# Expert layer's tokens without their bias, which is added where fetched rows are turned; one list product on ScalarE; the second tile's rows turned inside the first tile's first layer

## What is computed

```
h = x @ W_in + b_in                              # 2048 tokens, 256 -> 256
t = h.reshape(B * S, -1)
logits = t @ W_gate + b_gate                     # 8 experts
probs = jax.nn.softmax(logits, axis=-1)
topv, topi = jax.lax.top_k(probs, TOP_K)         # TOP_K = 2
topv = topv / jnp.sum(topv, axis=-1, keepdims=True)
route = jnp.zeros_like(probs).at[arange[:, None], topi].set(topv)
mid = jax.nn.relu(jnp.einsum('nd,edh->neh', t, W1) + b1)   # 256 -> 1024
eout = jnp.einsum('neh,ehd->ned', mid, W2) + b2            # 1024 -> 256
out = jnp.einsum('ne,ned->nd', route, eout) @ W_out + b_out
```

## Time and profile before

| | us |
|---|---|
| median of 3 timed runs | 1483.45 (1481.06 to 1484.49) |
| profiled execution, its own time | 1474.6 |
| its span in the trace | 1472.8 |
| cross-attention block, from first to last transpose back | 964.5 to 1104.3 |
| token projection and lists on PE | 1120.8 to 1146.4 |
| first transposes of fetched rows to end of first(0) | 1156.7 to 1168.0 |
| expert tiles from first(1) to the last product | 1171.2 to 1437.9 |

### The profile page before, as it was taken

The page is one execution under the profiler, slowest core; times in us unless marked ns, Lnnn a source line. Parts: engine busy times, 40 slices in busy tenths (PEclk is TensorE's granted clock), DMA queues, the critical chain, the costliest instruction groups (busy, mean ns, idle before and its releaser), DMA issues. The chain is left out here.

```text
span 1472.8 us, 27606 instructions
## 1 busy us (share of the span) xinstructions
PE 1311.2 (89%) x9707; PEld 1036.3 (70%) x9707; DVE 1016.0 (69%) x1992; ACT 877.4 (60%) x2193; POOL 465.7 (32%) x636
## 2 busy tenths in 40 slices
PE   5989999988699999968999766689989699999997
PEld 3534444435699999856888644478877599999995
DVE  5688787816456665555777896678875588888773
ACT  4436676674466666544121466477872588888873
POOL 5312221238233333432000356422110234444320
PEclk9999999999999999988999887599998799999998
DMA  4745224000000000021000300021202567777855
GB/s 88 225 77 155 45 53 76 6 5 1 30 2 1 2 2 1 2 93 29 1 1 1 81 16 1 22 56 42 50 16 76 176 215 230 236 233 231 232 161 184
DMA packets 97922, 116.16 MB, mean 79 GB/s; under 512 B 23552, under 2 KB 83193, under 8 KB 97785
## 3 DMA queue, kind: packets, MB, share of 16 engines
q1 hardware_dynamic: 88329, 99.84, 25.1%
q0 software_dynamic: 4416, 12.06, 2.7%
q10 hardware_dynamic: 5040, 2.49, 0.7%
HBM read 88.48 MB, written 16.55 MB: 71 GB/s over the span
## 5 line engine op out<-in xcount | busy, mean ns | idle before, releaser
L827 ACT ACTIVATE sa_probs<-ps 128x512 f32<-128x512 f32 (+1 forms) x304 | 154.3, 578 | 84.3 <-PE ps L780 83.2
L851 DVE TENSOR_REDUCE sa_top<-ps 128x2 f32<-128x1024 f32 (+3 forms) x160 | 171.4, 1115 | 37.7 <-PE ps L756 24.2
L3150 ACT ACTIVATE room<-ps,cx_top 128x154 f32<-128x154 f32 x256 | 97.2, 389 | 89.8 <-DVE cx_top L3214 89.8
L2688 PE MATMUL ps<-me_h,me_w_parts 128*128 128x256 f32 x1104 | 141.4, 289 | 4.2 <-DVE me_h L2774 4.2
L2688 PEld LDWEIGHTS ps<-me_h,me_w_parts 128*128 128x128 f32 x1104 | 138.0, 194 | 5.9 <-DVE me_h L2774 4.8
L2702 PE MATMUL ps<-me_w_parts,me_mid 128*128 128x256 f32 x1104 | 136.3, 283 | 0.0
L2702 PEld LDWEIGHTS ps<-me_w_parts,me_mid 128*128 128x128 f32 x1104 | 132.5, 188 | 0.0
L3012 POOL TENSOR_TENSOR room<-room 128x512 f32<-128x512 f32 x64 | 66.7, 1043 | 169.9 <-DVE room L3222 169.8
L2769 DVE TENSOR_TENSOR me_w_parts<-me_chunk,me_w_parts 128x1024 fp32r<-128x1024 f32 x92 | 110.4, 1222 | 13.2 <-ACT me_w_parts L2730 13.2
L2753 ACT ACTIVATE me_full<-ps,me_b 128x256 f32<-128x256 f32 x184 | 95.2, 517 | 40.5 <-PE ps L2688 40.5
L2798 DVE TENSOR_TENSOR me_mid<-me_full,me_mid 128x256 fp32r<-128x256 f32 x184 | 90.1, 507 | 41.3 <-ACT me_mid L2755 39.2
(11 more groups left out here) (472 smaller groups left out, 3437.0 us busy)
## 6 DMA issues: line engine op xcount, KB each, us to landing
me_chunk<-in_L_ffn_W_dram SPq DMA_DIRECT2D x92, 512.0 KB, 4.0
sa_k<-scr_k SPq DMA_DIRECT2D x48, 128.0 KB, 4.2
sa_q<-scr_q SPq DMA_DIRECT2D x96, 64.0 KB, 4.0
cn_qd<-cn_qh SPq DMA_DIRECT2D x60, 64.0 KB, 2.1
scr_q<-room SPq DMA_DIRECT2D x6, 512.0 KB, 4.3
scr_k<-room SPq DMA_DIRECT2D x6, 512.0 KB, 4.7
me_b<-in_L_ffn_b_dram SPq DMA_DIRECT2D x23, 128.0 KB, 4.3
x<-in_x_dram SPq DMA_DIRECT2D x4, 512.0 KB, 6.3
```

Source lines behind the costliest of these rows:

```text
L827: act.activation(probs[:, step % self.PROBS, h0:h0 + many, 0:w], src[:, :, 0:w], ACT.Exp, scale=DH ** -0.5).then_inc(exped.sem, 1)
L851: dve.tensor_reduce(top2[:, k % 2, k0 // 512, h0:h0 + many, sb % HBLK], src[:, :, 0:w], AX.X, ALU.max).then_inc(freed.sem, 1)
L2688: last = pe.matmul(ps[:, MID + n % 4, 0:RT], w[:, u % 2, 0, i, DM * k + P * b:DM * k + P * b + P], h[:, u % 2, j, k, :], start=(m == 0), s ...
L3150: last = act.activation(p[:, h + i, :], ps[:, S_BANK + n % SR, M * i:M * i + M], ACT.Exp, bias=top[:, t % 2, h + i:h + i + 1], accum_out=d ...
```

## The change

Four things are done.

- **b_in leaves the projection.** The load L2080, the tiles it needs, `bias_parts` on POOL and the sixteen products L2309 go. The tokens in `moe_tokens` are without b_in.
- **b_in is added in `take`.** ACT's one copy of 128x512 becomes two of 128x256 with a bias column per half k (`ACT.Identity` with `in_bias`), DVE's one subtraction becomes two `scalar_tensor_tensor` (turned row plus bias, minus high part). The semaphores count KD = 2 per tile.
- **The list product moves.** `mp_named` half 0 is made by ACT behind the copy of tile 13 (`t == NT - 3`) and no longer by DVE. The two small products on `mp_count` stand behind tile 3, not tile 4.
- **The second tile's rows are turned earlier.** turn(1) stands ahead of block 4 of first(0) on PE, and take(1) behind block 4 of tile 0 on ACT and DVE. All later tiles keep their places.

```
-    def bias_parts(self, pool):
...
-        then(pool.tensor_copy(self.ones_r[:, :], self.ones[0:3, :]))
...
-        then(pool.tensor_tensor(self.b_parts[:, :], self.b_in[:, :], self.term[:, :], ALU.add))
...
@@ Prepare.tensor
             for k in range(KD):
-                pe.matmul(bank, front.xt[:, k, P * t:P * t + P], front.w[:, k, 0:D], start=(k == 0), stop=False)
-            pe.matmul(bank, front.ones_r[:, :], front.b_parts[:, :], start=False, stop=True).then_inc(self.s["hidden"].sem, 1)
-            if t == 4:
+                last = pe.matmul(bank, front.xt[:, k, P * t:P * t + P], front.w[:, k, 0:D], start=(k == 0),
+                                 stop=(k == KD - 1))
+            last.then_inc(self.s["hidden"].sem, 1)
+            if t == 3:
@@ Prepare.scalar
+            if t == NT - 3:
+                act.wait_ge(self.s["hot_a"].sem, self.s["hot_a"].at(1))
+                act.activation(self.named[:, :, 0, :], self.one_a[:, :, :], ACT.Copy, scale=self.front.col[:, :]
+                               ).then_inc(self.s["scaled"].sem, 1)
@@ Prepare.vector
-        dve.wait_ge(self.s["hot_a"].sem, self.s["hot_a"].at(1))
-        dve.tensor_scalar(self.named[:, :, 0, :], self.one_a[:, :, :], self.front.col[:, :], None, ALU.mult
-                          ).then_inc(self.s["scaled"].sem, 1)
@@ moe_experts, tensor
                     for b in range(HB):
                         n = HB * u + b
+                        if n == HB // 2:
+                            turn(1)
...
                 first(0)
-                turn(1)
@@ moe_experts, scalar
-                    act.activation(h[:, u % 2, 0, :, :].rearrange("p k r -> p (k r)"), ps[:, TURN[u % 2], :],
-                                   ACT.Copy).then_inc(h_high.sem, 1)
+                    for k in range(KD):
+                        act.activation(h[:, u % 2, 0, k, :], ps[:, TURN[u % 2], RT * k:RT * k + RT], ACT.Identity,
+                                       bias=in_bias[:, k:k + 1]).then_inc(h_high.sem, 1)
...
-                        if b == HB - 1 and u + 1 < TILES:
+                        if b == (HB - 1 if u else HB // 2) and u + 1 < TILES:
                             take(u + 1)
@@ moe_experts, vector
-                    dve.tensor_tensor(h[:, u % 2, 1, :, :].rearrange("p k r -> p (k r)"), ps[:, TURN[u % 2], :],
-                                      raw(h[:, u % 2, 0, :, :]).rearrange("p k r -> p (k r)"),
-                                      ALU.subtract).then_inc(h_low.sem, 1)
+                    for k in range(KD):
+                        dve.scalar_tensor_tensor(h[:, u % 2, 1, k, :], ps[:, TURN[u % 2], RT * k:RT * k + RT],
+                                                 in_bias[:, k:k + 1], raw(h[:, u % 2, 0, k, :]), ALU.add, ALU.subtract
+                                                 ).then_inc(h_low.sem, 1)
```

More of the change, by code:

```diff
@@ L2053, in __init__ @@
         self.b_gate, self.b_logit = sb("b_gate", [P, E8]), sb("b_logit", [P, E8])
-        self.b_in, self.left, self.term = (sb(k, [3, D]) for k in ("b_in", "left", "term"))
-        self.high, self.b_parts, self.ones_r = sb("high", [3, D], F32R), sb("b_parts", [3, D], F32R), sb("ones_r", [3, P], F32R)
         self.w_t = sb("w_t", [P, KD, D])
@@ L2067, in begin @@
         self.s = {k: self.c.sig("mf_" + k) for k in (
-            "w_in", "b_sent", "made", "parts", "bias_turned", "bias_set", "b_cols_set", "w_turned", "w_t_set", "gate_made", "gate_set",
+            "w_in", "b_sent", "made", "bias_turned", "bias_set", "b_cols_set", "w_turned", "w_t_set", "gate_made", "gate_set",
             "varied", "rooted", "inverted", "shifted", "xn_dve", "xn_act", "turned", "xt_set", "logit", "logits")}
@@ L2084, in loaded @@
     def loaded(self, eng):
-        self.wait(eng, "w_in", 96)
+        self.wait(eng, "w_in", 80)
     def store_biases(self, sp, b1_cols):
@@ L2110, in constants @@
         self.constants_made = link.n
-    def bias_parts(self, pool):
[L2113 to L2119, removed]
-        then(pool.tensor_copy(self.ones_r[:, :], self.ones[0:3, :]))
[L2121 to L2128, removed]
-        then(pool.tensor_tensor(self.b_parts[:, :], self.b_in[:, :], self.term[:, :], ALU.add))
-        self.parts_made = link.n
     def bias_turn(self, pe):
@@ L2241, in done @@
         acts = sum(self.normal_engine(t) == "ACT" for t in range(NT))
-        for k, n in (("w_in", 96), ("b_sent", 16), ("made", self.constants_made), ("parts", self.parts_made), ("bias_turned", 1),
+        for k, n in (("w_in", 80), ("b_sent", 16), ("made", self.constants_made), ("bias_turned", 1),
                      ("bias_set", 1), ("b_cols_set", 1), ("w_turned", 1), ("w_t_set", 1), ("gate_made", 1), ("gate_set", 2),
@@ L2556, in moe_experts @@
         TERMS = ((0, 0), (1, 0), (0, 1))
+        in_bias = front.bias[:, E8 * HB:]
         SPLITS = {2: (0,), 5: (1,), HB - 1: (2, 3)}
@@ L2671, in turn @@
                     if u >= 2:
-                        pe.wait_ge(h_low.sem, h_low.at(u - 1))
+                        pe.wait_ge(h_low.sem, h_low.at(KD * (u - 1)))
                     for k in range(KD):
@@ L2679, in first @@
                 def first(u):
-                    pe.wait_ge(h_low.sem, h_low.at(u + 1))
+                    pe.wait_ge(h_low.sem, h_low.at(KD * (u + 1)))
                     pe.wait_ge(w_low.sem, w_low.at(chunk_at(0, u, 1) + 1))
@@ L2813, in moe_experts @@
             b_in[i].passed(32 * len(range(i, TILES, BUF)))
-        for s, k in ((turned, TILES), (h_high, TILES), (h_low, TILES), (w_high, 4 * TILES), (w_low, 4 * TILES),
+        for s, k in ((turned, TILES), (h_high, KD * TILES), (h_low, KD * TILES), (w_high, 4 * TILES), (w_low, 4 * TILES),
                      (mm, HB * TILES), (s_full, HB * TILES), (high, HB * TILES), (low, HB * TILES),
@@ L3717, in _ @@
                         front.constants(pool)
-                        front.bias_parts(pool)
             @block.tensor
```

3 lines of the change are left out of this document (1 added, 2 removed).

## The result

The changed kernel took **1468.55 us** (median; 1464.56 to 1471.55), the kernel before 1481.46 (1478.45 to 1484.49) on the same chip: ratio 0.9912, 95% interval 0.9889 to 0.9934, so 12.9 us or 0.9% faster.

A forecast was written before the change was run, and what follows sets the result against it. PE was taken to bound the expert tiles from first(1) on, so an earlier first(1) moves the rest. Terms -2.8 - 4.8 + 0.4 - 0.2 = -7.4 gave 1467.2, plus 8.9 carried over 1476.0 us; range 1472.0 to 1480.5.

The forecast's parts named there:

- The common sum: All four parts together: -2.8 - 4.8 + 0.4 - 0.2 = -7.4 us against the profiled execution's 1474.6.
- part 2: Projection without its sixteen bias products, list product moved to ACT: last token write 4.8 us sooner, lists not last.
- part 3: Bias added in take: take(0) 0.4 us longer on the path, hidden in the 21 later tiles.
- part 4: turn(1) and take(1) within first(0): first(1) released by the second chunk's split, -0.2 us, bounds -0.7 and +0.3.
- Carrying over the 8.9 us between profile and median: Adding before's difference between median 1483.45 and profiled execution to 1467.2, giving 1476.0 us.
- Part 1: Cross-attention tile 4 without POOL's ten instructions: whole excess of 2.77 us goes, -2.8; bound -1.6 for the wait alone.
- The others 0.31 of PE's queue each: Projection's sixteen bias products on PE: first 0.51, others 0.31 each, 5.2 us in all, 4.9 after the low clock.
- the lists: the rival: Ahead of POOL's first fetch, the lists or list product become last: +0.5 or +1.6, so 1476.5 to 1478.1; chance 0.12.
- if POOL is let in between: List stage, POOL's product running between DVE's steps: `mp_source` ready at 1143.2, ahead of the write landing at 1143.8.
- the estimate of 0.5 us for the move off DVE: List product by the skill's table: moving it off DVE worth 0.5 us; the prediction held 3.1 instead.
- block 4 not late: Bound of the early turn in first(0): without block 4's delay of 0.45 us, the gain is -0.7.
- its first rival: At first(1), the clock does not fall: extra 1.5 us lost, less about 0.5 waiting for ACT, 1475.0; chance 0.15.

The follow-up runs named there:

- e2: Changed kernel with the load of b_in and POOL's ten bias_parts instructions put back, result unused; 1471.96 us, ratio 0.9933 to the kernel before.
- e10: Kernel before with only the projection's sixteen bias products left out, so tokens lack b_in; 1474.01 us, ratio 0.9952 to the kernel before.
- e5: Changed kernel with a 3-row fp32r product of zeros put back in each projection tile; 1479.5 us, kernel before 1481.51.
- e4: Changed kernel without POOL's list product: DVE makes it from a list expanded to bf16, counts behind tile 2; 1470.26 us, ratio 0.9913 to the kernel before.
- e8: Changed kernel with the list product back on DVE ahead of the one-hot steps; 1472.05 us, ratio 0.9938 to the kernel before.
- e12: Changed kernel with e4's edit and tile 1's first weights loaded ahead of the last two token writes; 1473.9 us, ratio 0.9946 to the kernel before.
- e6: Changed kernel with a 128-row fp32r product of zeros put in each projection tile; 1470.32 us, kernel before 1481.51.
- e7: Changed kernel with a 3-row float32 product of zeros put in each projection tile; 1503.22 us, kernel before 1481.51.

## Why the prediction was right, and where it was wrong

- **The common sum.** It is short by 3.1 us of 10.5. By the table 1.2 of them lie ahead of the fetch (-6.0 and not -4.8, part 2), 1.3 between fetch and first(0) (-0.9 and not +0.4, part 3), 0.5 in part 4 and 0.7 behind it, and 0.6 came back ahead of the projection. Another 2.0 of the 7.4 us between 1476.0 and 1468.55 is before's median, which came out at 1481.46 and not 1483.45; the last 2.4 (12.9 - 10.5) lies within the measurement. Carrying over the 8.9 us between profile and median was sound for a difference of medians, but the changed kernel's own profile is 1.5 above its median: such an offset belongs to an execution.
- **Part 1, -2.8: right** to 0.02 us in the trace (e2), with the whole excess and not only the wait of 1.6. Something of the stretch behind it (+0.6) came back. It lies behind the last transpose back: the clock falls to 0.50 some 9.0 us behind that transpose in the changed kernel and 10.0 in the first trace of before. It is likely scatter: over the ten traces with a short tile 4 this stretch takes 122.1 to 123.6 us, over the four with a long one 122.7 to 123.0.
- **Part 2, the term that was mis-sized.** "The others 0.31 of PE's queue each" was the product's own time. The step that failed is that the rest of the tile stays at 1.06, that is, that a product costs its neighbours nothing: without it a tile took 0.88. The last write was due at -4.8 and came at about -7.4 (copy end 17.8 against 24.55 and 25.8; e10: 8.0 to 9.2). The sign stood in before's trace: its four products of a tile took 1.06 on the full clock, and its weight loads have the same gap of 0.33 as e5's, which I did not look for:

```profile
1136.33 0.18 PEld L2309 LDWEIGHTS ps<-mf_b_parts,mf_ones_r 3*128 3x128 f32 x1 [0.33 <-issue]
```

- **Part 2, the lists: the rival came true.** The forecast had `mp_source` 22.0 to 23.5 us after the projection's start; it came at 22.3 and 22.4. The forecast for the write was 23.0; it landed at 21.1. So the lists became last not because they were slower than reckoned, but because PE was faster, and the fetch moved by 6.0, not 7.4. The forecast's middle case, "if POOL is let in between", had `mp_source` at 1143.2, 22.4 behind the start, and that is what happened (e4): DVE, POOL, DVE by turns. Where the prediction says that the estimate of 0.5 us for the move off DVE (from the Trainium skill, "VectorE: DVE Perf Modes", section "The perf-mode tier table") does not hold here, it is the prediction that was wrong: POOL's turn of 2.66 stays on DVE's path either way, what goes is the rest of the 3.10, 0.4 us, and e8's fetch came 0.5 later. ACT's product took 1.51, forecast 1.46.
- **Part 3, +0.4: right for the take** (0.84 + 0.88 against 0.60 + 0.69, so +0.43), but the stretch as a whole fell by 0.9. The fetch's transfer took 4.45 instead of 5.15, with less traffic beside it (transfer engines busy for 0.79 and 0.74 in the windows above, before for 0.96 in the 3 us from 1151; e12 shows the effect by itself), and POOL's own instruction for it 1.22 instead of 1.79, for which no run shows the reason. The sum had treated both as fixed. In the 21 later tiles the take was hidden, as said: 261.9 us against 261.8, and no wait of PE.
- **Part 4, -0.2: releaser right, size -0.7**, my bound for "block 4 not late". The split ends 11.03 us after first(0)'s start and first(1) starts 0.1 later; before, it ended 1169.69 - 1159.26 = 10.43 after it. It comes 0.6 later where I had 0.75 for the take on ACT and 0.45 for block 4: the two don't add up.
- **The clock.** first(1) took 7.26, before 7.48: the low clock stayed, as the forecast had it against its first rival. It is also where the remaining -0.7 lies: from first(1) to second(0) before takes 7.68 and 8.73. This is scatter: of the ten traces with the early turn three (e6, e8, e12) take 8.7 to 8.8 there as well, the others 7.4 to 7.7, and those three are the ones with the shortest way from first(0) to first(1), 10.8 to 10.9.

## What to carry to other kernels

When a product with few rows stands among products with all 128, price it by the whole tile with and without it, and look in the weight loads for gaps: here it cost 0.5 us where its own row said 0.31. When several chains meet at one point, give each its own arrival before counting a gain, and remember that a gain larger than reckoned turns the second chain into the limit. And of a large product taken off VectorE only its own part is gained as long as GpSimd works beside it: here 0.5 us, where its row said 3.1, because most of that row was a wait for GpSimd.

## What the runs showed of the hardware that I had not expected

**TensorE busy without a break, at half clock.** In e7 the 3-row product is in float32 and takes 1.15 us, the four beside it 2.01. The window of e7 in the projection (columns as in the earlier trace rows):

```profile
1130.00:1140.00 10.00, 10.00 (x23) 5.56 (x22) 1.64 (x8) 1.15 (x3) 0.00 (x0) 0.50 0.15 51
1150.00:1160.00 10.00, 10.00 (x21) 5.03 (x19) 4.63 (x4) 1.15 (x3) 0.00 (x0) 0.50 0.49 171
```

PE is busy for 10.00 of 10 us, and the granted clock stays at 0.50 (1.2 GHz) in all four windows of 10 us that I read; the copy of the last tile ends 51.8 us after the start instead of 17.8, and the run takes 1503.2 us. In e5, with the same product in fp32r, the clock rose within the third tile. Sixteen such products cost some 30 us, three times what the whole change gave. Why the clock was not granted no run here tells; busy time in the profile is no sufficient sign for it.

**Shared access of VectorE and GpSimd.** One bf16 product of 1472 columns took 0.93 us on DVE with POOL idle (e4) and 3.10 beside POOL's; the first is a product of two tensors, the other one by a column. The Trainium skill, "GPSIMD Engine Reference", section "1. Specifications", names contention with VectorE instructions that have two inputs in SBUF or run in a mode with two ports. Here the records fit full exclusion by whole instructions: a step of 1.21 took 3.68 with POOL's product ahead of it, while the step before it (1.22) and the two behind it (1.21) were not slowed.
